# An attention and mixture-of-experts kernel: one list of eight per row in place of two, twelve second counts on VectorE, and image tokens of three batches embedded as one

## The reference

```python
tok = jnp.einsum('bnd,de->bne', patches, W) + b            # (64, 36, 768) x (768, 256)
h = jnp.concatenate([cls, tok], axis=1) + pos_embedding    # then layernorm, gamma, beta
h = jnp.concatenate([h, txt], axis=1)                      # (64, 165, 256)
...
topk = max(1, int(Tx * 0.3))                               # 49 of 165
scores = jnp.einsum('bhid,bhjd->bhij', q, k) * scale
topk_scores, indices = jax.lax.top_k(scores, topk)
masked = masked.at[bi, hi, ti, indices].set(topk_scores)   # -inf elsewhere
attn = jax.nn.softmax(masked, axis=-1)
...
h = h + _L0_attn_ref(_layernorm(h, axis=-1), ...)
h = h + _L0_ffn_ref(_layernorm(h, axis=-1), ...)           # router, top 8 of 64, shared and routed part
```

## Time and profile before

| | us |
|---|---|
| three runs, median (lowest, highest) | 3364.08 (3345.03, 3366.45) |
| the profiled execution, its own time | 3362.61 |
| its span, first to last instruction | 3360.9 |
| loop over batches, roughly | 0 to 2970 |
| experts | from about 2970 |

### The profile page before, as it was taken

How to read it: one execution, slowest core, us unless ns; L and a number is a source line. 1 busy time by engine, 2 the same in 40 slices (tenths; PEclk the granted TensorE clock), 3 DMA queues, 4 the chain that set the end, 5 groups by cost and what they waited for, 6 DMA issues and landing times.

```text
span 3360.9 us, 82985 instructions
## 1 busy us (share of the span) xinstructions
PE 2740.0 (82%) x22281; PEld 2098.7 (62%) x22281; DVE 2809.3 (84%) x11013; ACT 2785.1 (83%) x12673; POOL 2167.3 (64%) x3409
## 2 busy tenths in 40 slices
PE   4688888888888888888888888988888888647776
PEld 3466666666666666666666666666666666436665
DVE  1899999999999999999999999999999999822222
ACT  3999999999999999999999999999999999611111
POOL 3456767667676667767766676776676766444554
PEclk7899999999999998999999999999999999868888
DMA  1001100000000000000000000000000000016776
GB/s 51 11 14 20 20 21 21 21 21 20 14 20 20 21 21 21 21 15 19 20 20 21 21 21 21 18 17 20 20 21 21 21 20 17 11 38 158 174 176 139
DMA packets 181453, 116.34 MB, mean 35 GB/s; under 512 B 100208, under 2 KB 172484, under 8 KB 180964
## 3 DMA queue, kind: packets, MB, share of 16 engines
q1 hardware_dynamic: 146596, 91.60, 10.0%
q0 software_dynamic: 34368, 19.34, 3.9%
HBM read 66.51 MB, written 33.40 MB: 30 GB/s over the span
## 4 chain that ended last, share of the span: by engine, by line
DVE 38%; ACT 27%; PE 13%; issue 12%; DMA 4%; POOL 3%; DVEq 1%; SPq 1%; POOLq 0%; ACTq 0%
ACT JK L831 14%; DVE PR L1175 6%; DVE S L1028 5%; DVE ML L1070 5%; DVE MU L1047 4%; ACT E L819 4%; DVE XU L1037 4%; ACT SIDE L850 4%; DMA E<-x_rows,ids_t 2%; DMA out<-E,ids_t 2%; PE bank L1521 2%; DVE XL L1057 2%; PE bank L1676 1%; DVE RD L1180 1%; ACT PTT L861 1%
## 5 line engine op out<-in xcount | busy, mean ns | idle before, releaser
L831 ACT ACTIVATE JK<-S,thr 128x165 f32<-128x165 f32 x2688 | 1124.0, 442 | 3.4 <-POOL thr L562 1.7
L607 POOL DMA_INDIRECT slot_token<-TOKI,SLOT x512 | 541.3, 1057 | 202.8 <-issue 182.6
L850 ACT ACTIVATE SIDE<-S,t 128x165 f32<-128x165 f32 x1344 | 572.4, 447 | 9.4 <-POOL t L574 4.4
L831 ACT ACTIVATION_READ_ACCUMULATOR JK<-S,thr 128x1 f32 x2688 | 565.0, 210 | 0.0
L819 ACT ACTIVATE E<-bank,nb 128x165 f32<-128x165 f32 x1344 | 523.8, 418 | 14.6 <-DVE S L1028 14.4
L1175 DVE SCALAR_TENSOR_TENSOR PR<-S,TV,E 128x165 f32<-128x165 f32 x1344 | 434.1, 379 | 0.0
L1028 DVE TENSOR_SCALAR_CACHE_REDUCE S<-bank 128x165 f32<-128x165 f32 x1344 | 357.9, 314 | 12.5 <-PE bank L1504 10.5
L1047 DVE MAX8 MU<-XU 128x8 f32<-128x165 f32 x1344 | 349.2, 311 | 0.2 <-DVE XU L1037 0.2
L1070 DVE MAX8 ML<-XL 128x8 f32<-128x165 f32 x1344 | 339.7, 307 | 0.7 <-POOL XL L589 0.7
L1037 DVE SCALAR_TENSOR_TENSOR XU<-SIDE,S 128x495 f32<-128x495 f32 x448 | 317.0, 708 | 11.9 <-ACT SIDE L850 11.4
L589 POOL TENSOR_TENSOR XL<-SIDE,S 128x495 f32<-128x495 f32 x256 | 308.0, 1203 | 28.9 <-ACT SIDE L850 14.3
(11 more groups left out here) (196 smaller groups left out, 6981.8 us busy)
## 6 DMA issues: line engine op xcount, KB each, us to landing
S<-in_w_gate SPq DMA_DIRECT2D x64, 192.0 KB, 2.7
S<-in_w_up SPq DMA_DIRECT2D x64, 192.0 KB, 3.3
S<-in_w_down SPq DMA_DIRECT2D x64, 192.0 KB, 3.4
x_rows<-X SPq DMA_DIRECT2D x64, 160.0 KB
H<-in_txt SPq DMA_DIRECT2D x64, 128.0 KB, 5.9
QA<-QT SPq DMA_DIRECT2D x512, 10.3 KB
QB<-QT SPq DMA_DIRECT2D x512, 10.3 KB
out<-OT SPq DMA_DIRECT2D x64, 128.0 KB
```

The source lines that it names most:

```text
L607: pool.indirect_dma_start(slot_token, bass.IndirectOffsetOnAxis(SLOT[r % 2][:, 0, k:k + 1], 0), TOKI[r % 2][:, :], None, bounds_check=SLOT ...
L831: act.activation(JK[:, t % 4, :], S[r % 2][:, t, :], ACT.Sign, bias=(t0, t1)[n][:, t:t + 1], scale=-1.0, accum_out=(c0, c1)[n][:, t:t + 1] ...
L850: act.activation(SIDE[:, t % GROUP + GROUP * (g % 2), :], S[r % 2][:, t, :], ACT.Sign, bias=t2[r % 2][:, t:t + 1], scale=-1.0, accum_out=c ...
```

## The change: what it does

1. **Choice of the threshold.** The sign array is gone: `third_count` (ACT) writes its signs to a scratch tile `JL`, and only the count is used. From it DVE computes `off` and `turn` (+1 or -1: on which side of t2 the 49th lies; `side`, `side2`, for tiles 0 to 11 and 12 to 20). POOL `apart` makes (S - t2) * turn, one pass per tile, 21 per batch, in place of `under`. DVE `one_side` drives the wrong side out of the way, one instruction per group of 495 columns, and `nearest` takes one list of eight per row: 21 MAX8 in place of 42. The short instructions after it are rewritten. The slow branch stays; a row is sure if its 49th is at most the seventh or eighth entry of its side, by the side.
2. **Second counts.** Those of tiles 9 to 20 go from ACT to DVE (`second_count`, a comparison with an added-up result). `AHEAD` is 9: the halves are 0 to 8 and 9 to 20.
3. **Image tokens** of three batches are embedded as one, on 111 partitions, once in three iterations. The result stands in `HP`, from which a DMA per batch (`load_image`) brings 37 rows to `H`. Before the loop there are six more loads of weights and biases, and the patches of four batches are loaded ahead of the first text.
4. **Orders.** All five lists are rewritten.

```diff
 PACKED = 3
+TRIO = PACKED * IMG
+DEEP = 4
 NG = NT // GROUP
-AHEAD = 4 * GROUP
+AHEAD = 3 * GROUP
...
+            def load_patches(n):
...
+                for b in of_trio(n):
+                    at = IMG * ((b + PACKED - 1) % PACKED)
+                    sp.dma_start(PT[n % 2][:, :, at + 1:at + IMG], patches[bass.ds(b, 1), :, :, :].rearrange("a p k n -> p (a k) n"))\
+                        .then_inc(s_patch[n % 2], 16)
...
+            def load_image(b, r):
+
...
+                gated()
+                sp.wait_ge(s_gg, 4 * n + 4)
+                gated()
+                sp.dma_start(H[r][0:IMG, 1, :], HP[at:at + IMG, :]).then_inc(s_txt[r], 16)
...
             def refine2(i, r, half):
 
                 lo, hi = HALVES[half]
-                pool.wait_ge(s_cnt, CN * i + NT + hi)
-                gated()
-                pool.tensor_scalar(u1[:, lo:hi], c1[:, lo:hi], 0.5 * DAMP * SLOPE, DAMP * SLOPE * (T / 2 - AIM),
-                                   ALU.mult, ALU.add).then_inc(s_up, 1)
+                if half and SECOND:
+                    pool.wait_ge(s_cd, CD * (i + 1))
+                    scale, base = DAMP * SLOPE, -DAMP * SLOPE * AIM
+                else:
+                    pool.wait_ge(s_cnt, CN * i + NT + hi)
+                    scale, base = 0.5 * DAMP * SLOPE, DAMP * SLOPE * (T / 2 - AIM)
+                gated()
+                pool.tensor_scalar(u1[:, lo:hi], c1[:, lo:hi], scale, base, ALU.mult, ALU.add).then_inc(s_up, 1)
                 pool.wait_ge(s_up, UP * i + 15 + 3 * half)
                 pool.tensor_tensor(u2[:, lo:hi], u0[:, lo:hi], u1[:, lo:hi], ALU.add).then_inc(s_up, 1)
                 pool.wait_ge(s_up, UP * i + 16 + 3 * half)
...
-            def under(i, r, g):
-
-                pool.wait_ge(s_cnt, CN * i + 2 * NT + GROUP * (g + 1))
...
-                at = GROUP * (g % 2)
-                pool.tensor_tensor(XL[g % 3][:, :, :], SIDE[:, at:at + GROUP, :], S[r % 2][:, GROUP * g:GROUP * (g + 1), :],
-                                   ALU.mult).then_inc(s_xp, 1)
+            def apart(i, r, g):
+
+                n = NG * i + g
+                pool.wait_ge(s_turn, TN * i + 2 * [g in v for v in SETS].index(True) + 2)
+                if n >= DEEP:
+                    pool.wait_ge(s_list, GROUP * (n - DEEP + 1))
+                gated()
+                for t in range(GROUP * g, GROUP * (g + 1)):
+                    last = pool.tensor_scalar(X[n % DEEP][:, t % GROUP, :], S[r % 2][:, t, :], t2[r % 2][:, t:t + 1], turn[:, t:t + 1],
+                                              ALU.subtract, ALU.mult)
+                last.then_inc(s_xp, 1)
 
...
-            def side(i, r, g):
...
+            def third_count(i, r, g):
...
-                                   scale=-1.0, accum_out=c2[:, t:t + 1]).then_inc(s_cnt, 1)
+                for k in range(GROUP):
+                    t = GROUP * g + k
+                    n = NT * i + t
+                    if n >= 3:
+                        act.wait_ge(s_c2, n - 2)
+                    act.activation(JL[:, n % 3, :], S[r % 2][:, t, :], ACT.Sign, bias=t2[r % 2][:, t:t + 1],
+                                   scale=-1.0, accum_out=c2[:, t:t + 1]).then_inc(s_c2, 1)
...
+            def second_count(i, r, g):
+
+                if g == SECOND[0]:
...
+                for k in range(GROUP):
+                    t = GROUP * g + k
+                    n = CD * i + t - GROUP * SECOND[0]
+                    if n >= 3:
+                        dve.wait_ge(s_cd, n - 2)
+                    dve.tensor_scalar(JD[:, n % 3, :], S[r % 2][:, t, :], t1[:, t:t + 1], None, ALU.is_le, ALU.add,
+                                      accum_out=c1[:, t:t + 1]).then_inc(s_cd, 1)
...
+            def side(i, k):
...
+                dve.tensor_scalar(off[:, lo:hi], c2[:, lo:hi], 4.0, 4.0 * MIDDLE, ALU.mult, ALU.add).then_inc(s_turn, 1)
...
+            def side2(i, k):
...
+                dve.tensor_scalar(turn[:, lo:hi], off[:, lo:hi], 1.0, -1.0, ALU.min, ALU.max).then_inc(s_turn, 1)
...
+            def places2(i):
...
+                dve.scalar_tensor_tensor(ab[:, 1, :], turn[:, :], -8.0, ab[:, 0, :], ALU.mult, ALU.add).then_inc(s_turn, 1)
...
+            def one_side(i, g):
...
+                dve.scalar_tensor_tensor(X[n % DEEP][:, :, :], X[n % DEEP][:, :, :], -BIG, X[n % DEEP][:, :, :], ALU.mult, ALU.min)\
+                    .then_inc(s_x, 1)
...
+            def nearest(i, g):
...
                 for t in range(GROUP * g, GROUP * (g + 1)):
-                    dve.max(MU[:, t, :], XU[g % 2][:, t % GROUP, :]).then_inc(s_mu, 1)
...
+                    dve.max(LIST[:, 0, WIN * t:WIN * t + WIN], X[n % DEEP][:, t % GROUP, :]).then_inc(s_list, 1)
...
             def threshold(i):
 
-                dve.wait_ge(s_sel, SEL * i + 5)
-                dve.tensor_reduce(TV[:, :], A1[:, :, :], AX.X, ALU.min).then_inc(s_sel, 1)
+                dve.wait_ge(s_sel, SEL * i + 2)
+                dve.tensor_reduce(LV[:, :, :], GL[:, :, :].rearrange("p c (n k) -> p c n k", k=WIN), AX.X, ALU.min).then_inc(s_sel, 1)
...
+            def front_embed(n):
...
-                last.then_inc(s_fp, 1)
+                    last = pe.matmul(bF[0:TRIO, 0:D], PT[n % 2][:, k, :], WT[:, k, :], start=(k == 0), stop=(k == PK - 1))
+                last.then_inc(s_gp, 1)
```

More of the change, by code:

```diff
@@ L289, in parcels, with share, trio, of_trio @@
             return 16 * sum(m > 0 or at == PACKED - 1 for m in range(n % 2, n + 1, 2))
+        def share(i, groups, g):
+            return len(groups) * i + sum(k < g for k in groups)
+        TRIOS = (n_batch + PACKED - 1) // PACKED
+        def trio(m):
+            return m % PACKED == 0 and 0 <= m // PACKED < TRIOS
+        def of_trio(n):
+            return [b for b in range(PACKED * n - PACKED + 1, PACKED * n + 1) if b >= 0]
         def known(i):
@@ L906, in iteration @@
                 if has(i):
-                    exps(i, r, 2)
-                if has(i - 1):
-                    side(i - 1, (r - 1) % RING, 3)
+                    count(i, r, 0, range(0, AHEAD))
                 if has(i - 2):
@@ L1305, in iteration @@
                 if has(i - 1):
[L1306 to L1313 removed]
+                    one_side(i - 1, 0)
                 if has(i):
```

708 lines of the change are left out of this document (371 added, 337 removed).

## The result

The changed kernel takes 3753.38 us (median of four runs, 3743.71 to 3767.89), the kernel before beside it 3365.26 (3345.03 to 3377.54): ratio 1.116, 95% interval 1.110 to 1.123. It is 11.6% slower, where 4% faster was forecast. The profiled execution took 3743.71 us, its span 3742.0.

The account below looks back on a forecast made before the run. DVE bounds the kernel, ACT close beside; the change moves the bound to POOL, 41.4 us plus 1.0 of waits. Period 42.4, 2.35 less: 64 batches save 150 us, 8 are added before the loop, giving 3220 us, range 3090 to 3330.

Parts of the forecast that it names:

- the price of `apart`: POOL's 21 passes per batch, priced from the key centring at 0.49 us each, 10.3 us; ends 8.6 and 15.3.
- signs of being wrong: DVE waiting only for the branch; `apart` mean over 0.5 us; L607 DMA gaps under 0.36; image-DMA waits in `front_norm`.
- ACT: forecast 37.7 us busy: ACT per batch: 42.7 us less twelve second counts at 0.413, 5.0 us; with waits 39 to 40, no bound.
- DVE: forecast 39.3: DVE per batch: 44.1 us, including 1.65 for flag read and branch, less 4.8 net.
- the two ends that the prediction named: Price of a DVE second count: 0.243 us (`take`) or 0.35 (L995); the nearer taken, 2.9 us for twelve.
- the forecast's sum: POOL per batch: 38.2 us it can't shed, less 4.8 products and 2.3 image step, plus 10.3 passes: 41.4.
- Before the loop 8 us were forecast: Before the loop: 8 us more, estimated, for six loads, patches of four batches and one hop for first tokens.
- POOL isn't the bound: Rival: POOL's DMA gaps shrink or passes cost 0.41; DVE sets the period, 40.0 us, 3065 us; chance 0.15.
- Slower, by collisions on POOL: Rival: passes take 0.80 us, period 48.9, 3636 us; decides from 0.60 us per pass; chance 0.10.
- Handovers: Rival: passes at 0.54 us and 2 us of waits between engines, period 44.5 us, 3355 us; chance 0.13.
- The slow branch, as computed: Rival: the list misses a 49th, 80 us per branch; recomputed counts say it shouldn't run, by one place; chance 0.02.
- The rule that spoke against the change: Two-input DVE and SBUF-reading POOL instructions exclude each other; 0.3 us lost per pass gives 6.3 us, period 48.7.

Follow-up runs that it names:

- e6: The kernel before, with POOL's key centring subtracting the mean instead of adding its negative; ratio 1.007.
- e5: Also written e5_add: the changed kernel, each `apart` pass adding -t2, made by DVE, instead of subtracting t2; 3135.51 us, ratio 0.933.
- e1: The changed kernel, with the second number per row in `apart` replaced by the constant 1.0 and the slow branch closed; 3616.38 us, ratio 1.074.
- e3: The kernel before, with the key centring's constant factor read from a column, so two numbers per row; 3365.05 us, ratio 0.999.
- e17: The kernel of e10 unchanged, run a third time, on a chip that didn't stretch PE's context matmuls; 3197.42 us, ratio 0.950.
- e16: The kernel of e5, with V's matmuls on PE placed between the context's sums and values; 3375.01 us, ratio 1.002.
- e7: The kernel of e5, with the second counts of tiles 9 to 20 back on ACT; 3741.04 us, ratio 1.104.
- e10: The kernel of e5, with -t2 made by POOL in `refine2` instead of by DVE; 3546.71 us, ratio 1.047.
- e12: The kernel of e10 unchanged, run again on the same chip as e11; 3539.94 us, ratio 1.041.
- e11: The kernel of e5 unchanged, run again on another chip; 3519.34 us, ratio 1.035.

## Why the prediction was wrong, step by step

**The step that failed** is the price of `apart`: "The nearest row is the key centring, of the same width ... I take 0.49, 10.3 us", with 0.73 as the upper end. The row was near in width, engine, arrays in and type, and not in the operation: it adds. With `subtract` in place of `add` the very row goes from 402 to 850 ns (e6), and the pass from 910 to 464 with `add` in place of `subtract` (e5). The second number per row, which the forecast left at nothing, is 0.07 to 0.08 us of it (e1, e3). At 986 ns in the mean, 21 passes are 20.7 us and not 10.3. The bound from both sides was too narrow for a form with no row: both ends came from the same row, undisturbed and disturbed, and none from another operation. Two of the signs of being wrong that the prediction named are in the change's trace: the mean of `apart` over 0.5 us, and the gap before the DMAs at L607's place (L662) under 0.36 us, 0.32.

**The rest of the sum.** Put the measured 0.98 in place of 0.49 and the forecast's period is 42.4 + 21 x 0.49 = 52.7 us; 50.96 was measured. With e5_add the other terms can be read.

ACT: forecast 37.7 us busy, measured 2206.80/58 = 38.0.

DVE: forecast 39.3 with the 1.65 us of the branch, measured 2267.30/58 = 39.1, of which 0.9 are the two instructions for -t2 (468 ns each). Two errors cancel there. The counts cost 12 x 0.305 = 3.7 us and not 2.9: between the two ends that the prediction named, 0.243 and 0.35, a little nearer to the far one. A nearer row was there: in the timeline of the kernel before eight masks, also 165 columns from SBUF, take 2.47 us, 0.31 each. And the idle time before the first instruction behind the branch, 95.9 us in the earlier trace rows, has no counterpart: in e5_add's loop the idle time by `issue` before all of DVE's groups is under 1 us; why isn't shown.

POOL: its busy time is 33.9 us, its waits for other engines 112.8/58 = 1.9, so that it couldn't shed 39.4 of 41.35 us, with passes of 590 ns in the mean (12.4 us). By the forecast's sum it would have been 38.2 - 4.8 - 2.3 + 12.4 = 43.5. That is four us too much: the gaps and durations of POOL's other work were counted as fixed, and they aren't. A packed DMA costs (158.3 + 32.4)/155 = 1.23 us in e5_add against 1.75 before, a DMA of eight 1.34 against 1.42; together 2.1 us per batch. Some 1.1 us more are in the short instructions of `guess` and `refine` and 0.4 in the two sums at `H` (the one of 37 rows took 1.15 us in the median before and takes 0.72). The groups of e5_add's steady loop, columns as above:

```profile
L646 POOL TENSOR_SCALAR X<-S,nt,turn 128x165 f32<-128x165 f32 x1218 | 703.9, 590 | 39.5 <-DVE nt L1130 36.7 <-issue 0.6
...
L665 POOL DMA_INDIRECT slot_token<-TOKI,SLOT x466 | 481.7, 1034 | 158.3 <-issue 141.9 <-ACT JK L893 16.5
...
L1150 DVE SCALAR_TENSOR_TENSOR X<-X 128x495 f32<-128x495 f32 x406 | 272.6, 671 | 8.8 <-POOL X L646 1.6
...
L688 POOL DMA_INDIRECT slot_token<-PACKI,PACK x155 | 158.3, 1021 | 47.5 <-issue 32.4 <-POOL packf L678 9.7 <-ACT E L881 5.5
```

Before the loop 8 us were forecast, and e5_add's first reciprocal is 6.6 us later than before (162.2 against 155.6). The change's own is 25.2 later, with slow passes ahead of it.

**The rivals.** "POOL isn't the bound", with its shrinking DMA gaps, is the nearest to what e5_add shows: the gaps did shrink, and the time is between its 3065 us and the forecast's 3220. But that DVE then sets the period isn't shown. Of 41.35 us DVE is busy for 39.1 and POOL can't shed 39.4, each waits about 2 us, DVE for the most part for POOL and POOL for DVE, and e17, which puts work of DVE on POOL, is slower. "Slower, by collisions on POOL" had the right engine, the right sign and, at 0.80 per pass, most of the size (3636), but the wrong mechanism: in the change the shortest of 1344 passes takes 910 ns. Its threshold, 0.60 us per pass, was drawn too low: e5_add has 0.59 in the mean, for which the forecast's sum gives 44.5 us and no gain, and its period is 41.35, since POOL's other work shrank by about 4 us. "Handovers" is what e16 shows, up to 3.6 us per batch from PE's order alone, the clock's part in it open. The slow branch, as computed, didn't run: its lines have no row.

**The rule that spoke against the change.** In e5_add, 355 of 1344 passes take over 0.6 us, and 314 of these overlap a `one_side` of DVE for over 0.1 us; of the 989 shorter ones 77 do. This trace agrees with the Trainium skill, SBUF — State Buffer, "Who interferes with whom", for DVE's instruction with two arrays in: the collisions are there. The line of passes is busy for 776.3 us in the whole span, which is 134 us above 1344 passes of the median, 0.478; so they cost POOL 2.1 us per batch, and not the 6.3 that the rule gave with every pass losing 0.3. The row that the prediction took for the rule, L1013, is no case of it: `XN` has one array in. The trace shows it longer beside POOL's product all the same. In the kernel before 46 of its 64 start while the product at L589 runs, take 0.90 us or more and end after it; the 16 that start first take 0.38 to 0.39, and the product 1.30. In the change, without that product, all take 0.41.

**The two other parts of the change.** Twelve second counts on DVE: on the stretching chips e7, with them on ACT, is 194 us above e10, 3.0 us per batch, in the same job, and e10 itself is no faster than e5_add (e12 beside e11). So that part pays there, a little less than the 3.7 us that the expectation of e7 gave; how much on an unstretched chip wasn't measured. The image step of three batches wasn't taken out alone. Its share of e5_add's gain is open.

## What to carry to other kernels

Price an instruction from a row with the same engine, form and operation; where only the operation differs, measure it by itself before 21 of them go on an engine that is to become the bound. On POOL write `x - c`, with c a number per row, as `x + (-c)`. And look at the minimum of a group before calling it contention: a floor above the neighbour's median is the instruction, a long tail over a short median is the neighbour.
